# Decay attention: masked scores copied to SBUF a step ahead, second softmax weighing a step later, nine filler matmuls a step

## The reference, cut to what matters

```python
scores = q @ k.T / sqrt(8)                        # causal, 128 x 128
p_     = softmax(where(mask, scores, -1e32)) * mask
dist   = sqrt(clip((p_.sum(-1) - cumsum(p_)) * |i - j|, 0))
effect = clip(exp(dist * -softplus(gamma)), 1e-5, 1e5)
p      = softmax(where(mask, scores * effect, -1e32))
out    = p @ v                                    # row 0 set to zero
```

## Time and profile before

| | |
|---|---|
| three runs | 3229.29, 3239.71, 3274.91 us; median 3239.71 |
| profiled execution | 3245.55 us, its span 3243.8 us |
| granted TensorE clock, mean of the span | 0.848 |
| busy: PE, DVE, ACT, POOL | 2771.9, 1960.9, 1513.2, 1261.0 us |
| decay attention: first and last of 128 scans start | 1827.5 and 3023.6 us |

### The profile page before, as it was taken

How to read it: one execution, slowest core, us unless ns; L and a number is a source line. 1 busy time by engine, 2 the same in 40 slices (tenths; PEclk the granted TensorE clock), 3 DMA queues, 4 the chain that set the end, 5 groups by cost and what they waited for, 6 DMA issues and landing times. The chain is left out here.

```text
span 3243.8 us, 60046 instructions
## 1 busy us (share of the span) xinstructions
PE 2771.9 (85%) x21812; PEld 1904.3 (59%) x21812; DVE 1960.9 (60%) x3888; ACT 1513.2 (47%) x2961; POOL 1261.0 (39%) x1551
## 2 busy tenths in 40 slices
PE   7998699992999999999997687888888888888476
PEld 6887477772555555555554465565555555555365
DVE  4995477775444454444444567666776677676624
ACT  1442366663333332233222366666666666666442
POOL 5661244443100000000000366655665666565371
PEclk9996699995999999999998568767887787686587
DMA  1110000000000000000000000000000000000002
GB/s 42 39 41 4 7 2 2 2 2 24 1 1 0 0 0 0 0 0 0 0 0 21 1 1 2 1 1 1 2 1 1 1 2 1 1 2 1 4 1 53
DMA packets 31576, 21.60 MB, mean 7 GB/s; under 512 B 24553, under 2 KB 28649, under 8 KB 31364
## 3 DMA queue, kind: packets, MB, share of 16 engines
q0 software_dynamic: 6144, 9.84, 1.3%
q1 hardware_dynamic: 25220, 8.94, 1.2%
HBM read 14.58 MB, written 4.19 MB: 6 GB/s over the span
## 5 line engine op out<-in xcount | busy, mean ns | idle before, releaser
L1245 DVE TENSOR_TENSOR prod<-c_h,act 128x512 f32<-128x512 f32 x352 | 243.4, 692 | 481.0 <-PE c_h L1097 439.0
L1177 ACT ACTIVATE act<-c_h 128x512 f32<-128x512 f32 x352 | 210.2, 597 | 655.9 <-PE c_h L1097 655.9
L1428 POOL TENSOR_TENSOR d_decay<-d_later,d_posg 128x768 f32<-128x768 f32 x128 | 232.6, 1817 | 437.5 <-DVE d_later L1827 437.5
L1124 PE MATMUL c_out<-e_w,hid 128*128 128x64 f32 x2816 | 388.7, 281 | 0.1
L1124 PEld LDWEIGHTS c_out<-e_w,hid 128*128 128x128 f32 x2816 | 340.6, 191 | 79.5 <-issue 79.3
L1071 POOL TENSOR_TENSOR x_rest<-flatT,x_hm 64x512 f32<-64x512 bf16 (+1 forms) x33 | 38.2, 1156 | 748.8 <-ACT x_hm L1157 724.8
L1469 PE MATMUL d_T<-ident,d_p 128*128 128x128 f32 x768 | 165.7, 336 | 184.2 <-ACT d_pT L1603 104.5
L1827 DVE TENSOR_TENSOR_SCAN d_later<-d_cont,d_ex 128x768 f32<-128x768 f32 x128 | 225.1, 1759 | 73.8 <-ACT d_ex L1621 73.8
L1097 PE MATMUL c_h<-x_hm,e_w_hh 128*128 128x512 bf16 x704 | 267.5, 380 | 0.9 <-ACT wT L1170 0.9
L1097 PE MATMUL c_h<-x_hm,e_w_mm 128*128 128x512 bf16 x704 | 267.6, 380 | 0.0
L1097 PE MATMUL c_h<-x_hl,e_w_lh 128*128 128x512 bf16 x704 | 267.4, 380 | 0.0
(11 more groups left out here) (356 smaller groups left out, 6287.5 us busy)
## 6 DMA issues: line engine op xcount, KB each, us to landing
out_h<-g_Y SPq DMA_DIRECT2D x8, 512.0 KB, 4.0
rows<-in_table,idx POOLq DMA_INDIRECT x128
e_w<-in_e_w SPq DMA_DIRECT2D x2, 704.0 KB
d_cont<-in_d_cont SPq DMA_DIRECT2D x1, 384.0 KB
e_w<-in_e_w SPq DMA_DIRECT2D x1, 352.0 KB
d_conv<-in_d_conv SPq DMA_DIRECT2D x1, 320.0 KB
d_wqk<-in_d_wqk SPq DMA_DIRECT2D x1, 256.0 KB
d_pos<-in_d_pos SPq DMA_DIRECT2D x1, 192.0 KB
```

The source lines that it names most:

```text
L1124: last = nc.tensor.matmul(bo[:, b * D:(b + 1) * D], hid[u][:, b * P:(b + 1) * P], w2[:, c, :], start=(c == 0 and b == 0), stop=(c == NCH - ...
L1177: nc.scalar.activation(act1[u][:], b1[u][:], ACT.Silu).then_inc(S["activated"], 1)
L1245: nc.vector.tensor_tensor(prod[u][:], b3[u][:], act1[u][:], ALU.mult).then_inc(S["multiplied"], 1)
L1428: pool.tensor_tensor(decay[u][:], later[u][:, 0:2 * SEG].rearrange("p (e s) -> p e s", e=2), posg[:, h:h + 2, :], ALU.mult).then_inc(U["pl ...
```

## The change

- Four SBUF tiles `d_kept` are new. ACT copies each score tile into one of them; DVE's maxima, subtractions and decay product read `d_kept` where they read `d_S` in PSUM. A PSUM score tile is free as soon as it is copied.
- PE issues the scores of step K + 1 in turn K, and ACT copies them in the same turn.
- DVE's decay product and second maxima come a turn later (step K - 2 in turn K) and stand before the scan; before, they stood behind it.
- POOL's subtraction of the second maxima moves behind the group's work. ACT's turn begins with the copy of the transposed block, and its exponential of `d_p` comes last.
- Filler comes in bursts of three: behind the scores, behind the first transposes, and once more each turn (behind the second transposes in even turns, behind the transposes back in odd ones). That is nine a step in place of four.

The core of the diff:

```diff
-    KEEP_V, KEEP_P, KEEP_T = 3, 3, 8
-    WARM = 4
+    KEEP_V, KEEP_S, KEEP_P, KEEP_T = 3, 4, 3, 8
+    WARM = 3
...
+        kept = [m_.sb(f"d_kept{u}", [P, 2, SEG]) for u in range(KEEP_S)]
...
+                        h = 2 * ((K - 1) % PAIRS)
+                        pool.wait_ge(U["scanned"], K)
+                        if K - 1 >= 2:
+                            pool.wait_ge(U["weighed"], K - 2)
+                        pool.tensor_tensor(decay[u][:], later[u][:, 0:2 * SEG].rearrange("p (e s) -> p e s", e=2),
+                                           posg[:, h:h + 2, :], ALU.mult).then_inc(U["placed"], 1)
...
-                    if step_there(K - 2):
-                        u, w = (K - 2) % 2, (K - 2) % KEEP_P
-                        pool.wait_ge(U["max2_made"], 2 * (K - 1))
-                        pool.tensor_tensor(long(p2[w]), long(p2[w]), wide(mx2[u], 1, P), ALU.subtract)
-                        pool.tensor_tensor(short(p2[w]), short(p2[w]), wide(mx2[u], 0, HALF), ALU.subtract)\
-                            .then_inc(U["shifted2"], 1)
...
-                    if step_there(K):
-                        u = K % 2
-                        h = 2 * j
-                        pool.wait_ge(U["scanned"], K + 1)
-                        if K >= 2:
-                            pool.wait_ge(U["weighed"], K - 1)
-                        pool.tensor_tensor(decay[u][:], later[u][:, 0:2 * SEG].rearrange("p (e s) -> p e s", e=2),
-                                           posg[:, h:h + 2, :], ALU.mult).then_inc(U["placed"], 1)
+                    if step_there(K - 2):
+                        u, w = K % 2, (K - 2) % KEEP_P
+                        pool.wait_ge(U["max2_made"], 2 * (K - 1))
+                        pool.tensor_tensor(long(p2[w]), long(p2[w]), wide(mx2[u], 1, P), ALU.subtract)
+                        pool.tensor_tensor(short(p2[w]), short(p2[w]), wide(mx2[u], 0, HALF), ALU.subtract)\
+                            .then_inc(U["shifted2"], 1)
...
-                        pe.wait_ge(U["weighed"], K - 1)
+                        pe.wait_ge(U["S_kept"], K - 1)
...
+                def keep_warm():
+                    for _ in range(WARM):
+                        nc.tensor.matmul(bO[:], ident_b[:], fill[:], start=True, stop=True)
...
+                    if step_there(K + 1):
+                        scores(K + 1)
                     if step_there(K):
-                        scores(K)
                         if quad_there((K - 6) // 2):
                             pe.wait_ge(Q["attT_kept"], (K - 6) // 2 + 1)
-                        for _ in range(WARM):
-                            nc.tensor.matmul(bO[:], ident_b[:], fill[:], start=True, stop=True)
+                        keep_warm()
                     if step_there(K - 3):
                         turn(K - 3, 0)
+                        keep_warm()
                     if j == 0:
...
+                        if K % 2 == 0:
+                            keep_warm()
...
                         last.then_inc(Q["back"], 1)
+                        keep_warm()
...
+                    if step_there(K - 3):
+                        keep_turned(K - 3, 0)
+                    if step_there(K):
+                        act.wait_ge(U["shifted"], 2 * (K + 1))
+                        nc.scalar.activation(ex[K % 2][:], ex[K % 2][:], ACT.Exp).then_inc(U["exped"], 1)
...
-                    if step_there(K):
-                        act.wait_ge(U["shifted"], 2 * (K + 1))
-                        nc.scalar.activation(ex[K % 2][:], ex[K % 2][:], ACT.Exp).then_inc(U["exped"], 1)
-                    if step_there(K - 1):
-                        u = (K - 1) % 2
-                        act.wait_ge(U["root_done"], K)
-                        nc.scalar.activation(decay[u][:], decay[u][:], ACT.Exp, scale=-1.0).then_inc(U["decay_made"], 1)
-                    if step_there(K - 3):
-                        keep_turned(K - 3, 0)
-                    if step_there(K - 2):
-                        w = (K - 2) % KEEP_P
-                        act.wait_ge(U["shifted2"], K - 1)
-                        nc.scalar.activation(p2[w][:], p2[w][:], ACT.Exp).then_inc(U["exped2"], 1)
                     if j == 0:
                         n = m + 1
...
+                    if step_there(K + 1):
+                        act.wait_ge(U["scored"], K + 2)
+                        if K + 1 >= KEEP_S:
+                            act.wait_ge(U["weighed"], K + 2 - KEEP_S)
+                        nc.scalar.activation(kept[(K + 1) % KEEP_S][:], bS[(K + 1) % 2][:, :, 0:SEG], ACT.Copy)\
+                            .then_inc(U["S_kept"], 1)
+                    if step_there(K - 1):
+                        u = (K - 1) % 2
+                        act.wait_ge(U["root_done"], K)
+                        nc.scalar.activation(decay[u][:], decay[u][:], ACT.Exp, scale=-1.0).then_inc(U["decay_made"], 1)
...
+                    if step_there(K - 2):
+                        w = (K - 2) % KEEP_P
+                        act.wait_ge(U["shifted2"], K - 1)
+                        nc.scalar.activation(p2[w][:], p2[w][:], ACT.Exp).then_inc(U["exped2"], 1)
...
-                        dve.wait_ge(U["scored"], K + 1)
-                        if K >= 2:
-                            dve.wait_ge(U["exped"], K - 1)
-                        nc.vector.tensor_reduce(mx[u][:, 1], long(bS[u]), AX, ALU.max).then_inc(U["max_made"], 1)
-                        nc.vector.tensor_reduce(mx[u][:, 0], short(bS[u]), AX, ALU.max).then_inc(U["max_made"], 1)
+                        dve.wait_ge(U["S_kept"], K + 1)
+                        nc.vector.tensor_reduce(mx[u][:, 1], long(kept[K % KEEP_S]), AX, ALU.max).then_inc(U["max_made"], 1)
+                        nc.vector.tensor_reduce(mx[u][:, 0], short(kept[K % KEEP_S]), AX, ALU.max).then_inc(U["max_made"], 1)
                         dve.wait_ge(U["max_made"], 2 * K + 1)
                         if K >= 2:
                             dve.wait_ge(U["scanned"], K - 1)
-                        nc.vector.tensor_tensor(long(ex[u]), long(bS[u]), wide(mx[u], 1, P), ALU.subtract)\
+                        nc.vector.tensor_tensor(long(ex[u]), long(kept[K % KEEP_S]), wide(mx[u], 1, P), ALU.subtract)\
                             .then_inc(U["shifted"], 1)
                         dve.wait_ge(U["max_made"], 2 * K + 2)
-                        nc.vector.tensor_tensor(short(ex[u]), short(bS[u]), wide(mx[u], 0, HALF), ALU.subtract)\
+                        nc.vector.tensor_tensor(short(ex[u]), short(kept[K % KEEP_S]), wide(mx[u], 0, HALF), ALU.subtract)\
                             .then_inc(U["shifted"], 1)
                     i = (K - 6) // 2
...
+                    if step_there(K - 2):
+                        u, w = K % 2, (K - 2) % KEEP_P
+                        dve.wait_ge(U["decay_made"], K - 1)
+                        if K - 2 >= KEEP_P:
+                            dve.wait_ge(U["turned"], 2 * (K - 1 - KEEP_P))
+                        nc.vector.scalar_tensor_tensor(p2[w][:], decay[u][:], 1e-5, kept[(K - 2) % KEEP_S][:],
+                                                       ALU.max, ALU.mult).then_inc(U["weighed"], 1)
+                        dve.wait_ge(U["weighed"], K - 1)
+                        if K - 2 >= 2:
+                            dve.wait_ge(U["shifted2"], K - 3)
+                        nc.vector.tensor_reduce(mx2[u][:, 1], long(p2[w]), AX, ALU.max).then_inc(U["max2_made"], 1)
+                        nc.vector.tensor_reduce(mx2[u][:, 0], short(p2[w]), AX, ALU.max).then_inc(U["max2_made"], 1)
...
-                    if step_there(K - 1):
-                        u, w = (K - 1) % 2, (K - 1) % KEEP_P
-                        dve.wait_ge(U["decay_made"], K)
-                        if K - 1 >= KEEP_P:
-                            dve.wait_ge(U["turned"], 2 * (K - KEEP_P))
-                        nc.vector.scalar_tensor_tensor(p2[w][:], decay[u][:], 1e-5, bS[u][:, :, 0:SEG],
-                                                       ALU.max, ALU.mult).then_inc(U["weighed"], 1)
-                        dve.wait_ge(U["weighed"], K)
-                        if K - 1 >= 2:
-                            dve.wait_ge(U["shifted2"], K - 2)
-                        nc.vector.tensor_reduce(mx2[u][:, 1], long(p2[w]), AX, ALU.max).then_inc(U["max2_made"], 1)
-                        nc.vector.tensor_reduce(mx2[u][:, 0], short(p2[w]), AX, ALU.max).then_inc(U["max2_made"], 1)
...
```

2 lines of the change are left out of this document (1 added, 1 removed).

## The result

| | before | changed |
|---|---|---|
| median of the runs on the same chip | 3234.50 us (4 runs) | 3348.86 us (4 runs, 3336.24 to 3376.69) |
| ratio to before | 1 | 1.037 (95% interval 1.028 to 1.047) |
| profiled execution, its span | 3245.55, 3243.8 us | 3340.92, 3339.1 us |
| granted clock, mean of the span | 0.848 | 0.878 |
| stage: interval between two scans | 9.42 us | 10.08 us |

The changed kernel is slower by 3.7%. 127 x (10.08 - 9.42) = 84 us of the 95 us between the two spans lie between the first and the last scan. Of the rest 2 us lie ahead of the first scan and 9 behind the start of the last, and I did not follow those. TensorE's clock was higher on average, and the kernel slower all the same. Medians in this text are of all runs of a kernel; ratios compare only the runs within 1.5% of that kernel's fastest, since some runs are up to 3% longer.

What follows compares the result with a forecast made beforehand. Before: engine-to-engine waits bound full-clock steps, PE half-clock ones (46% of the time). After: the VectorE-POOL lock at full clock, 9.0 us a step; 127 x (9.42 - 9.0) = 53 us off 3245.55 gives 3192 us, range 3090 to 3325.

Steps and rivals of the forecast that it cites:

- the one on filler: Five more matmuls a step on PE, hidden at full clock (7.4 us under 9.0), keep nearly all the stage there.
- rival C: Clock still falls, in odd turns between bursts: 12.9 us a step while low, 3278 to 3377 us; chance 0.20.
- Full clock, lock: VectorE and POOL exclude each other on SBUF operands in the stage: 9.0 us a step at full clock.
- floor of 8.55: Shortest step the VectorE-POOL lock allows, 8.55 us, if POOL works in every moment VectorE leaves free.
- ceiling of 9.5: Step of 9.5 us if POOL's free time during the second maxima is lost in each step.
- The 8.40 I set out from: Full-clock step of the kernel before, 8.40 us, from a four-step group of 33.59 us at clock 0.94.
- Clock: Stage at full clock: steps of 11 to 12 us disappear, which is the gain against the 9.42 us mean.
- Copy: New ScalarE copy of scores to SBUF: 0.83 us a step, hidden with ScalarE at about 7.5 us under 9.0.
- the sign of D: Score copy delayed by ScalarE's q work, 3256 to 3294 us, chance 0.10; sign: `d_kept` waits over 0.5 us a step.
- Moved work: Scores a step ahead: VectorE's 226.8 us wait goes; the longer way from subtraction to scan is covered by moved work.
- Operands: VectorE reading SBUF instead of PSUM: nothing counted, since a maximum took 691 ns from PSUM and 686 from SBUF.
- Rival B: No lock on these VectorE instructions; ScalarE, PE and the `d_y` wait bound: 3030 us, half way 3110; chance 0.15.

Runs made afterwards that it cites:

- experiment 7: The changed kernel with filler in bursts of four, twelve a step in place of nine: 3298.02 us, ratio to before 1.010.
- experiment 9: The changed kernel with nine fillers in place of three behind the scores in even turns, twelve a step on average: 3234.69 us, ratio to before 0.999.
- experiment 6: The changed kernel with VectorE's first maxima and subtractions reading PSUM again and bursts of four, twelve fillers a step: 3116.86 us, ratio to before 0.954.
- experiment 1: The changed kernel with VectorE's first maxima and subtractions reading the scores in PSUM again, nine fillers a step: 3116.76 us, ratio to before 0.951.

## Why the prediction was wrong

**The step that failed** is the one on filler: "So I expect the full clock in nearly all of the stage." It was low for 34% of it. My rival C had the place in part, and its 3278 to 3377 hold the result: 12.9 us for a step at half clock (13.01 measured), and by its own sum with 34% and the full-clock step of experiment 7, 1 / (0.66 / 9.11 + 0.34 / 12.9) = 10.1 us (10.08 measured). That this sum comes out so well is partly luck. It prices all time at 1.2 GHz as if it were the convolution's step, but the 13.01 us step is itself only half at the low clock (0.75), and the 8.91 us step loses nothing at 0.93; the convolution's step happens to be 32% of the group's time, near the 34% of the low share. C got 0.20, though the rows pointed to it: the wait for `d_y` in the earlier trace rows lies in an even turn, between the burst behind the scores and the first transposes, and none of the new bursts fills it. I wrote that no stretch between two bursts is longer than "a few transposes and a wait", and did not ask how long that wait becomes when VectorE's subtractions, which stand ahead of `d_y`, are held by POOL. I put C's place in the odd turns. That is where the clock fell before the change: 41 of 55 falls in the stage stand behind a wait for ScalarE's copy of the transposes (`d_pT`). In the changed kernel both falls of a group begin in even turns, behind `d_y`, and the wait for `d_attT` at the end of an odd one comes second, as experiment 9 shows.

The sum, term by term:

- *Full clock, lock:* 9.0 forecast, 9.11 measured with three fillers more (experiment 7). It lies between the floor of 8.55 and the ceiling of 9.5, but 9.0 was their middle and not worked out, so the closeness is partly luck. With the subtractions out of the lock it is 8.34 with the same filler (experiment 6), so the lock on these two instructions is 0.8 us a step at full clock. The 8.40 I set out from is not quite full clock: the group's clock is 0.94, and its last step took 8.99 us at 0.76, where other groups have 7.93 at 1.00. The full-clock step before was 8.13.
- *Clock:* I booked 9.42 - 8.40 = 1.0 us a step as gained by a clock that no longer falls. Measured from full clock, the low clock cost 9.42 - 8.13 = 1.3 us a step before and still costs 10.08 - 9.11 = 1.0: a third less time at 1.2 GHz, but the steps it meets are dearer by the filler in them. So the step lost 1.0 us to lock and filler at full clock and got back 0.3 from the clock: 127 x 0.7 is near the 84 us measured. As the 9.11 is with twelve fillers, the split is an estimate.
- *The lock's second price:* at nine fillers the lock costs 10.08 - 8.16 = 1.9 us a step (experiment 1), more than twice the 0.8 us at full clock. The rest goes with the clock: 34% low with the lock, 14% without.
- *Copy:* 0.83 us forecast, 0.81 measured. It is not wholly hidden: VectorE waits 71.7 us for `d_kept`, 0.56 a step, a little over the 0.5 I had set as the sign of D; but in experiment 1, where the step is 1.9 us shorter, it waits 82.8 us for it. In which steps this is on the path I did not separate.
- *Moved work:* the wait for scores (226.8 us) went, as forecast. The longer way from subtraction to scan is real: the first transposes hold ScalarE's copy for 354 us, and the exponential of `d_ex` stands behind it (before: 76 us).
- *Operands:* maxima 685 to 691 ns from either memory, as forecast. The Trainium skill ("VectorE: DVE Perf Modes", § The TRN2 errata) has a difference of 62 cycles between PSUM and SBUF, and no row here shows it: the subtraction is 681 ns from PSUM and 680 at least from SBUF.
- *Rival B* (no lock) fell with the durations. B's 3030 to 3110 is near what its remedy gives: 3117 with PSUM inputs on two of three instructions.

The Trainium skill ("SBUF — State Buffer", § SBUF: two separate sides) says which pairs of instructions exclude each other, and the runs agree in each: two SBUF inputs on VectorE wait (1695 ns), one PSUM input doesn't (681), one input alone doesn't (685). Another rule spoke for the change: "VectorE: DVE Perf Modes" of the Trainium skill (§ Rules for kernel authors) offers copying from PSUM to SBUF first where many operations follow. Here five instructions followed. The version of experiment 1 keeps the copy and is 5% faster than before; two of the copy's readers, the subtractions (the maxima keep their durations), make the difference between a ratio of 1.037 and one of 0.951.

What stays open: how nine fillers would do at full clock, which no group of the changed kernel shows, and why the changed kernel settles on a group of exactly 40.96 us with two falls in each, rather than a mixture as in experiment 7. I did not try to shift it without a change of its work.

## What to carry to other kernels

Before moving an operand of a two-input VectorE instruction from PSUM to SBUF, add up what VectorE and GpSimd would then hold exclusively in a step: here 3.78 + 5.80 us, against a step of 8.4, gave warning of the loss at full clock and bounded it (8.55 to 9.5; 9.11 measured with twelve fillers). Where the clock is not at its full level throughout, price each regime by itself, and check filler against the longest wait of the changed schedule and not of the old one; in this schedule a middling amount was worse than less or more, since it made the half-clock steps longer without ending them (9 a step: +3.7%; 4: level; 15: level). That isn't a rule for other schedules: with the subtractions from PSUM 6, 9 and 12 are all 5% faster than before, and 4 is level. And look where the filler stands: in the old order it stands ahead of the scores that VectorE waits for, and there 15 a step held the clock and gained nothing. Last, free a PSUM tile by a copy, but let instructions with a second SBUF input keep reading PSUM while it lasts.

## What the runs showed of the hardware

- A small tile read with a broadcast counts as a second input: L1804's median of 1695 ns is with `d_mx`, 128 x 4 elements.
- The loser of the lock still saves part of its time: L1804 ended 0.55 us after POOL's L1382 (alone 0.68), L1386 0.90 after L1804 (1.04), L1807 0.29 after L1386 (0.41), L1387 0.46 after L1807 (0.61). That is 0.12 to 0.15 each time.
- A loop can settle on one pattern with the clock's changes: with nine fillers the group takes 40.96 us in 27 of 31 groups of the changed kernel (clock 0.83), and 40.96 in 17 of 31 groups of the kernel before with nine (clock 0.79), though order and operands differ. That the clock's changes set this length is my reading; no run tests it.
- At the low clock, PE busy 3.41 of 3.41 us with convolution and projections stayed low for two such stretches. The Trainium skill ("TensorE: Matmul & The Clock Gate", § Part 4) says that the full clock does not engage for transposes; here the instructions were matmuls in fp32, which that section does not speak of, so this row neither supports nor refutes it.
